# A graph-attention layer on one NeuronCore: the running sums move from a TensorE product and a ScalarE copy to two VectorE additions

## The chip, the core and the metric

The kernel runs on one core of one Trainium2 chip. The metric is the device time of one execution in microseconds (us). TensorE multiplies matrices, VectorE and ScalarE work on tiles in SBUF and PSUM, GpSimd issues the gathers, SyncE issues the other transfers. Each engine takes its instructions in order, and semaphores tie the engines together. In the profile they are called PE (PEld for its weight loads), DVE, ACT, POOL and SP (SPq for the queue that issues transfers).

## What is computed

A layer of 6250 nodes with 256 features (8 heads of 32) is the sum of a graph attention over 206250 edges sorted by destination, a linear-attention mixer, and after that eight experts. The stage that the change touches is the graph attention:

```
h_src, h_dst = h[src], h[dst]                      # h = layernorm(x) @ W.T, per edge
alpha = einsum(h_src, a_src) + einsum(h_dst, a_dst)
enc   = relu(edge_attr @ edge_W.T + edge_b)
alpha = leaky(alpha + sum(enc * h_dst))
ex    = exp(alpha - segment_max(alpha, dst)[dst])
out   = segment_sum(h_src * ex / segment_sum(ex, dst)[dst], dst)
```

## The kernel before

The program runs in stages: a start stage (`stage_start`), the mixer (`stage_kv`, `stage_mix`), the edge stage (`stage_edges`, 884 to 2835 us of the profile), `stage_combine` and `stage_experts`. The edge stage is unrolled by hand; nothing but the order of the code and the semaphores sets its order.

Edges are sorted by destination and cut into steps of 256 edges that touch 64 destination nodes. A **turn** is two steps (512 edges), there are 452 turns, and eight turns are a **window** (57 of them). At turn tau the front half of the work is done for tau, and the back half for d = tau - 12 (`LAG` is 11); the segment maximum and the exponentials of a finished window are worked out in its four following turns, one link of the chain in each (k = 0 to 3, k being the turn's place in the window).

In one turn the engines do this, in this order:

- TensorE: `spread_out` (L1666, L1670) spreads the destination rows over the edges with the one-hot tile `hot`; `encode` of the next turn (L1655) multiplies `w_rows` by `feat`, 30 rows (3 of ones for the bias, 27 of edge features in three bf16 parts); `aggregate(d)` (L1702, L1706) sums the weighted source rows `rows` per destination into `ps_a`; `reduce` (L1683) sums the products per head. In `aggregate`, step 0 of a turn goes on from what `sums` holds: the identity product L1702 first brings that tile (128x264, float32) into `ps_a`, except at k = 0.
- VectorE: `multiply` (L1851, two instructions), `spreader` (L1840, one-hot row tile `hot` of the next turn, 128x512 bf16), `weigh` (L1934), `add(d, 1)` (L1927, adds step 1 of `ps_a` to `sums`), and the links of the chain. `add(d, 0)` runs on VectorE for k = 0 alone, behind `rescale` (L1911, L1915).
- ScalarE: `rectify` (L1748), `put_back` (L1801, copies step 0 out of `ps_a` into `sums`, k > 0), `take_src` (L1759), `put_exps` (L1785), `one_hot` (L1793, L1795), and the exponentials of the chain.
- GpSimd: four gathers (L1643) for each turn whose rows were not gathered in earlier stages, 1312 in all; `released` holds each back until a turn has come. SyncE: `load_pair` (rows of `relb` and `feat` for two turns), two tiles of `table` a turn, and the loads of a window.

Which tile of `sums` a step adds to is a number read from `turns_w` into a register (`value_load`). `aggregate(d)` waits until both sums of d - 1 have been added (`added`), `reduce` waits for `multiply`, and `spread_out` stands behind `reduce` on TensorE.

## Time and profile before

| what | us |
|---|---|
| median of 3 runs (3996.34 to 3997.9) | 3997.06 |
| the profiled execution | 3997.66 |
| its span | 3995.8 |
| TensorE busy | 3671.8 (92%) |
| VectorE busy | 2677.7 (67%) |
| ScalarE busy | 2308.9 (58%) |
| GpSimd busy | 1792.8 (45%) |

The busy shares are means over stages with different limits. The profile also has the busy time by stretches of time, instructions in order of time, groups of instructions by line, and the clock that TensorE was granted, 1.00 being 2.4 GHz and 0.50 being 1.2 GHz.

### The profile page before, as it was taken

How to read it: one execution, taken by the hardware profiler on the slowest of the kernel's cores; microseconds unless marked ns; L12 is line 12 of the kernel's file. 1: busy time of each engine (PE TensorE's matmuls, PEld its weight loads, DVE VectorE, ACT ScalarE, POOL GpSimd, SP SyncE). 2: the span in 40 equal slices, each digit the busy share in tenths (PEclk: the TensorE clock that was granted, in tenths of full speed). 3: DMA queues.
4: the chain of work that ended last, by engine and by line, in shares of the span. 5: the costliest groups of instructions: out<-in, count | busy, mean ns of one | idle time of the engine just before them, and what ended most of it. 6: DMA issues, size and time to landing. Idle time of an engine off the chain costs nothing. (4 is left out here: it accounts for less than half of the span.)

```text
span 3995.8 us, 80425 instructions
## 1 busy us (share of the span) xinstructions
PE 3671.8 (92%) x22765; PEld 1800.7 (45%) x22765; DVE 2677.7 (67%) x5470; ACT 2308.9 (58%) x6074; POOL 1792.8 (45%) x1859
## 2 busy tenths in 40 slices
PE   5599989978999999999999999999699999999999
PEld 3344433323443344434444444443366666666666
DVE  8399933338898999989989898988533333332323
ACT  4466555545777777777777777777333333333332
POOL 4177766656666666666666666665000000000000
PEclk8799999987999999999999999999659999999999
DMA  7677767767777777777777777776220000000000
GB/s 217 168 216 217 217 217 229 231 196 222 214 228 217 222 221 223 224 220 218 227 221 223 219 229 218 224 222 196 66 74 1 10 10 0 9 9 0 9 9 9
DMA packets 378173, 629.74 MB, mean 158 GB/s; under 512 B 83912, under 2 KB 245063, under 8 KB 377536
## 3 DMA queue, kind: packets, MB, share of 16 engines
q1 hardware_dynamic: 277266, 356.80, 28.1%
q0 software_dynamic: 93408, 257.23, 24.3%
q10 hardware_dynamic: 7104, 11.01, 0.8%
q8 instruction: 179, 2.93, 0.3%
q14 instruction: 216, 1.77, 0.1%
HBM read 520.59 MB, written 104.12 MB: 156 GB/s over the span
## 5 line engine op out<-in xcount | busy, mean ns | idle before, releaser
L1643 POOL DMA_INDIRECT s_rows<-scratch_src_rows,s_idx_w x1312 | 1270.5, 968 | 656.5 <-issue 398.6
L1851 DVE SCALAR_TENSOR_TENSOR s_enc<-s_enc,s_a_dst,s_ps_d 128x512 f32<-128x512 f32 x904 | 633.2, 742 | 104.2 <-PE s_ps_d L1670 92.8
L2299 DVE SCALAR_TENSOR_TENSOR kx_y_all<-e_ps_o,kx_gate,kx_y_all 128x256 f32 (+1 forms) x392 | 173.6, 480 | 684.4 <-PE e_ps_o L2354 684.4
L1934 DVE TENSOR_TENSOR s_rows<-s_rows,s_ps_x 128x1024 f32<-128x1024 f32 x452 | 546.5, 1209 | 22.2 <-ACT s_a_w L1779 22.1
L1748 ACT ACTIVATE s_enc<-s_ps_f 128x1024 f32<-128x1024 f32 x452 | 460.2, 1018 | 160.2 <-PE s_ps_f L1655 152.4
L1706 PE MATMUL s_ps_a<-s_rows,s_hot_e 128*64 128x264 f32 x3616 | 536.6, 421 | 2.9 <-DVE s_rows L1934 2.9
L1793 ACT ACTIVATE s_hot_e<-k_iota_row,s_rel_w 128x64 f32<-128x64 f32 x1808 | 480.2, 338 | 0.0
L2313 ACT ACTIVATE ke_sums<-e_ps,kx_b,kx_g 128x448 f32<-128x448 f32 x224 | 162.1, 724 | 513.1 <-PE e_ps L2333 513.1
L1702 PE MATMUL s_ps_a<-ke_sums,k_ident 128*128 x790 | 292.4, 453 | 105.0 <-DVE ke_sums L1927 64.7
L2333 PE MATMUL e_ps<-kx_xT,ke_sums 128*128 (+1 forms) x896 | 348.1, 542 | 6.2 <-PEq L180 6.2
L2354 PE MATMUL e_ps_o<-ke_sums 128*128 128x256 f32 x1568 | 347.6, 379 | 0.0
L2343 PE MATMUL e_ps<-ke_sums 128*128 128x448 f32 x896 | 345.9, 539 | 0.0
L1706 PEld LDWEIGHTS s_ps_a<-s_rows,s_hot_e 128*64 128x64 f32 x3616 | 229.4, 142 | 251.3 <-issue 159.0
L2354 PEld LDWEIGHTS e_ps_o<-ke_sums 128*128 128x128 f32 x1568 | 297.8, 190 | 58.6 <-issue 20.9
L1683 PE MATMUL s_ps_s<-s_enc,s_head_sum 128*32 128x256 f32 x3616 | 304.7, 410 | 10.7 <-DVE s_enc L1851 4.0
L1801 ACT COPY ke_sums<-s_ps_a 128x264 f32 x395 | 148.0, 375 | 284.0 <-PE s_ps_a L1706 283.0
L1655 PE MATMUL s_ps_f<-s_feat,k_w_rows 30*128 30x512 bf16 x904 | 276.7, 386 | 19.7 <-DMA s_feat<-scratch_step_parts 19.2
L1195 POOL DMA_INDIRECT m_rows<-scratch_src_rows,m_idx x248 | 235.1, 948 | 117.9 <-issue 65.0
L1091 POOL DMA_INDIRECT n_rows<-scratch_src_rows,n_idx x248 | 235.4, 949 | 109.0 <-issue 71.9
L1670 PE MATMUL s_ps_d<-s_hot,s_table 128*128 128x256 bf16 x1808 | 283.6, 281 | 0.0
L1265 ACT ACTIVATE m_feats<-m_ps_s 124x896 f32<-124x896 f32 x224 | 193.3, 915 | 144.1 <-PE m_ps_s L1207 144.1
L2319 ACT ACTIVATE ke_sums<-e_ps,kx_b,kx_g 128x448 f32<-128x448 f32 x224 | 162.1, 724 | 174.6 <-PE e_ps L2343 174.6
(280 smaller groups left out, 5084.6 us busy)
## 6 DMA issues: line engine op xcount, KB each, us to landing
s_table<-scratch_dst_parts SPq DMA_DIRECT2D x904, 96.0 KB
s_rows<-scratch_pre_rows SPq DMA_DIRECT2D x124, 528.0 KB
s_relb<-scratch_rel_rows SPq DMA_DIRECT2D x226, 256.0 KB
scratch_pre_rows<-n_rows SPq DMA_DIRECT2D x62, 528.0 KB
scratch_pre_rows<-m_rows SPq DMA_DIRECT2D x62, 528.0 KB
s_rows<-scratch_src_rows,s_idx_w POOLq DMA_INDIRECT x1312
s_feat<-scratch_step_parts SPq DMA_DIRECT2D x226, 54.0 KB
s_pen_w<-scratch_pen_rows SPq DMA_DIRECT2D x228, 48.1 KB
```

What stands on the lines that cost most here:

```text
L1643: pool.indirect_dma_start(out=rows[:, d % R, m, :], out_offset=None, in_=scr["src_table"], in_offset=bass.IndirectOffsetOnAxis(ap=idx_w[:, ...
L1670: last = PE.matmul(ps_d[:, c, sub * GE:(sub + 1) * GE], table[:, u, sub, c * P:(c + 1) * P], hot[:, v, sub * GE:(sub + 1) * GE], start=Fal ...
L1683: last = PE.matmul(ps_s[32 * b:32 * (b + 1), :], head_sum[:, 28 - 4 * k:60 - 4 * k], enc[:, d % 2, c, sub * GE:(sub + 1) * GE], start=(k = ...
L1702: PE.matmul(ps_a[:, 0, 0:SRC_W], keep["ident"][:], sums[:, bass.ds(j, 1), :].rearrange("p o w -> p (o w)"), start=True, stop=False, skip_g ...
L1706: last = PE.matmul(ps_a[t * WN:(t + 1) * WN, sub, 0:SRC_W], hot_e[:, d % 3, 2 * sub + t, :], rows[:, d % R, 2 * sub + t, :], start=(sub == ...
L1748: A.activation(enc[:, d % 2], ps_f[:], ACT.Relu).then_inc(enc_made, 1)
L1793: A.activation(hot_e[:, d % 3, m, :], keep["iota_row"][:, 0:WN], ACT.Abs, bias=rel_w[:, w % 3, k * TD + m:k * TD + m + 1]).then_inc(dist_m ...
L1851: V.scalar_tensor_tensor(out=enc[:, d % 2, c, :], in0=enc[:, d % 2, c, :], scalar=a_dst[:, c:c + 1], in1=ps_d[:, c, :], op0=ALU.add, op1=A ...
L1934: V.tensor_tensor(v, v, by.unsqueeze(3).to_broadcast([P, TD, H, HD]), ALU.mult).then_inc(weighed, 1)
L2333: last = nc.tensor.matmul(ps[q][:, 0:W], w["W1"][:, e, c, m * P:(m + 1) * P], keep["xT"][:, c, bass.ds(i * 2 * W + hf * W, W)], start=(c = ...
L2343: last = nc.tensor.matmul(ps[q][:, 0:W], w["W2"][:, e, c, m * P:(m + 1) * P], h1[:, c, hf * W:(hf + 1) * W], start=(c == 0), stop=(c == 1))
L2354: last = nc.tensor.matmul(ps_o[q][:, r, :], h2[:, c, b * P:(b + 1) * P], w["Wo"][:, e, c, :], start=(c == 0), stop=(c == 1))
```

## The change

All of it is in the edge stage, but for the zeroed tiles.

- `aggregate` has no identity product any more; both steps of a turn come out of `ps_a` alone. `put_back` on ScalarE is gone, and `add(d, 0)` runs on VectorE in every turn, so that VectorE adds twice a turn and reads a register twice a turn.
- `spreader` works on pairs of turns: one 128x1024 instruction in every second turn, for a pair that is one to two turns ahead; `hot` has twice the size, and SyncE loads `relb` a pair ahead of `feat`.
- Steps of the chain leave VectorE: `starts` (the two small tiles `first`), `keep_run`, `fall` and `factors` (was L1911) run on ScalarE, and `both_ends` is one instruction and not two.
- `feat` and `w_rows` have 128 rows, of which 98 are zeros, so that `encode` contracts over 128 rows; `b_rows` and the tile of ones of the mixer's two bias products have 128 rows and not 3. The tiles are cleared once, in the start stage and at the head of the edge stage.

```diff
@@ aggregate (TensorE)
-                    if k > 0:
-                        j = pe.value_load(turns_w[0:1, w % 4, KS + 2 * k:KS + 2 * k + 1], min_val=0, max_val=NJ - 1)
...
-                    if k > 0:
-                        PE.matmul(ps_a[:, 0, 0:SRC_W], keep["ident"][:], sums[:, bass.ds(j, 1), :].rearrange("p o w -> p (o w)"),
-                                  start=True, stop=False, skip_group_check=True)
@@ ScalarE
+                def starts(w):
+                    act.wait_ge(hot_made, KW // 2 * w + 1)
+                    wait(act, fac_made, w - 2)
+                    h = hot[:, KW // 2 * w % 2, 0, 0:1]
+                    A.copy(first[:, w % 2, 0:1], h)
+                    A.activation(first[:, w % 2, 1:2], h, ACT.Identity, scale=-1.0, bias=one[:, 0:1]).then_inc(first_made, 1)
+                def keep_run(w):
...
+                def fall(w):
...
+                def factors(w):
+                    act.wait_ge(turned_, w + 1)
...
-                def put_back(d):
-                    w, k = win(d)
-                    j = act.value_load(turns_w[0:1, w % 4, KS + 2 * k:KS + 2 * k + 1], min_val=0, max_val=NJ - 1)
-                    act.wait_ge(summed[0], d + 1)
-                    A.copy(sums[:, bass.ds(j, 1), :].rearrange("p o w -> p (o w)"), ps_a[:, 0, 0:SRC_W]).then_inc(added, 1)
@@ VectorE
+                V.memset(feat[:], 0.0).then_inc(cleared, 1)
...
-                def spreader(d):
...
+                def spreader(g):
+                    dve.wait_ge(rel_in[g % RP], 16 * (g // RP + 1))
+                    wait(dve, spread[1], 2 * (g - 1))
+                    if g >= 2 and (g - 2) % (KW // 2) == 0:
+                        dve.wait_ge(first_made, (g - 2) // (KW // 2) + 1)
+                    V.tensor_scalar(hot[:, g % 2], relb[:, g % RP], p64[:, 0:1], None, ALU.is_equal).then_inc(hot_made, 1)
...
-                    if tau + 1 < D:
-                        spreader(tau + 1)
+                    if tau % 2 == 1 and tau + 3 < D:
+                        spreader((tau + 3) // 2)
...
-                    if tau >= LAG + 1 and win(tau - LAG - 1)[1] == 0:
+                    if tau >= LAG + 1:
                         add(tau - LAG - 1, 0)
```

TensorE, one plain turn (no link of the chain in it). Before:

```order
L1666 MATMUL s_ps_d<-s_hot,s_table 128x256 x4
L1670 MATMUL s_ps_d<-s_hot,s_table 128x256 x4
L1655 MATMUL s_ps_f<-s_feat,k_w_rows 128x512 x2
L1696 TENSOR_LOAD s_turns_w
L1696 ISA x2
L1702 ISA
L1702 MATMUL s_ps_a<-ke_sums,k_ident 128x264
L1706 MATMUL s_ps_a<-s_rows,s_hot_e 64x264 x4
L1683 MATMUL s_ps_s<-s_enc,s_head_sum 32x256 x4
```

The same turn after:

```order
L1674 MATMUL s_ps_d<-s_hot,s_table 128x256 x4
L1678 MATMUL s_ps_d<-s_hot,s_table 128x256 x4
L1663 MATMUL s_ps_f<-s_feat,k_w_rows 128x512 x2
L1709 MATMUL s_ps_a<-s_rows,s_hot_e 64x264 x4
L1691 MATMUL s_ps_s<-s_enc,s_head_sum 32x256 x4
```

The register read and the identity product are gone; nothing else moved.

VectorE, one plain turn. Before:

```order
L1851 SCALAR_TENSOR_TENSOR s_enc<-s_enc,s_a_dst,s_ps_d 128x512 x2
L1840 TENSOR_SCALAR s_hot<-s_relb,s_p 128x512
L1934 TENSOR_TENSOR s_rows<-s_rows,s_ps_x 128x32x32
L1920 TENSOR_LOAD s_turns_w
L1920 ISA x2
L1927 ISA
L1927 TENSOR_TENSOR ke_sums<-s_ps_a,ke_sums 128x264
```

An odd plain turn after (an even one has no L1868):

```order
L1874 SCALAR_TENSOR_TENSOR s_enc<-s_enc,s_a_dst,s_ps_d 128x512 x2
L1868 TENSOR_SCALAR s_hot<-s_relb,s_p 128x1024
L1937 TENSOR_LOAD s_turns_w
L1937 ISA x2
L1944 ISA
L1944 TENSOR_TENSOR ke_sums<-s_ps_a,ke_sums 128x264
L1951 TENSOR_TENSOR s_rows<-s_rows,s_ps_x 128x32x32
L1937 TENSOR_LOAD s_turns_w
L1937 ISA x2
L1944 ISA
L1944 TENSOR_TENSOR ke_sums<-s_ps_a,ke_sums 128x264
```

A second register read and a second addition now stand between the one-hot rows and L1951 (`weigh`).

## Rows read from the trace of the kernel before

**Rows 1.** The page: the span of the profiled execution.
```profile
span 3995.8 us, 80425 instructions
```

**Rows 2.** Busy time by stretch: a start of the stage, its middle, one clock dip.
```profile
core 0: us, PE busy (x) PEld busy (x) DVE busy (x) ACT busy (x) POOL busy (x), PEclk, DMA share, GB/s
...
904.00:925.30 21.30, 19.37 (x98) 5.72 (x97) 19.02 (x25) 5.96 (x11) 16.12 (x18) 0.50 0.80 235
...
1400.00:2600.00 1200.00, 1119.87 (x8434) 482.40 (x8432) 1088.67 (x2112) 927.00 (x2717) 803.31 (x832) 0.97 0.77 222
...
2044.87:2048.28 3.41, 3.41 (x21) 1.11 (x20) 1.94 (x6) 2.02 (x8) 2.80 (x3) 0.50 0.79 230
```

**Rows 3.** Timeline (start, length, work, idle before): TensorE in turns 15 and 451.
```profile
949.29 0.39 PE L1666 MATMUL s_ps_d<-s_hot,s_table 64*128 64x256 bf16 x4
...
2791.86 0.39 PE L1666 MATMUL s_ps_d<-s_hot,s_table 64*128 64x256 bf16 x4
```

**Rows 4.** Timeline: TensorE through one plain turn.
```profile
2033.74 0.39 PE L1666 MATMUL s_ps_d<-s_hot,s_table 64*128 64x256 bf16 x4
...
2035.13 0.71 PE L1702 MATMUL s_ps_a<-ke_sums,k_ident 128*128 x2
...
2035.78 1.11 PE L1706 MATMUL s_ps_a<-s_rows,s_hot_e 128*64 128x264 f32 x8
...
2036.82 0.64 PE L1683 MATMUL s_ps_s<-s_enc,s_head_sum 128*32 128x256 f32 x8
...
2037.39 0.39 PE L1666 MATMUL s_ps_d<-s_hot,s_table 64*128 64x256 bf16 x4
```

**Rows 5.** Timeline: VectorE through one plain turn, from the addition before it.
```profile
2027.16 0.43 DVE L1927 TENSOR_TENSOR ke_sums<-s_ps_a,ke_sums 128x264 f32 x1
2027.50 1.40 DVE L1851 SCALAR_TENSOR_TENSOR s_enc<-s_enc,s_a_dst,s_ps_d 128x512 f32<-128x512 f32 x2
...
2028.82 0.35 DVE L1840 TENSOR_SCALAR s_hot<-s_relb,s_p 128x512 bf16<-128x512 bf16 x1
2029.08 1.21 DVE L1934 TENSOR_TENSOR s_rows<-s_rows,s_ps_x 128x1024 f32<-128x1024 f32 x1
...
2030.21 0.43 DVE L1927 TENSOR_TENSOR ke_sums<-s_ps_a,ke_sums 128x264 f32 x1
...
2030.91 1.41 DVE L1851 SCALAR_TENSOR_TENSOR s_enc<-s_enc,s_a_dst,s_ps_d 128x512 f32<-128x512 f32 x2 [0.27 <-PE s_ps_d L1670]
```

**Rows 6.** Groups by line (busy us, mean ns, idle before): moved work, contraction rows, gathers.
```profile
L1643 POOL DMA_INDIRECT s_rows<-scratch_src_rows,s_idx_w x1312 | 1270.5, 968 | 656.5 <-issue 398.6 <-PE s_ps_a L1706 137.5 <-DVE s_hot L1840 55.5
...
L1655 PE MATMUL s_ps_f<-s_feat,k_w_rows 30*128 30x512 bf16 x904 | 276.7, 386 | 19.7 <-DMA s_feat<-scratch_step_parts 19.2
...
L906 PE MATMUL n_ps_qk<-kn_b_rows,kn_ones 3*128 3x512 bf16 x49 | 19.1, 389 | 0.3 <-DVE n_kp L1020 0.3
...
L1911 DVE TENSOR_SCALAR s_fac<-s_ps_x,s_first 128x8 f32<-128x8 f32 x56 | 15.6, 279 | 0.0
...
L1826 DVE MEMSET s_feat<- 3x2048 bf16 x1 | 1.8, 1765 | 5.6 <-PEq L180 5.6
```

**Rows 7.** Timeline: TensorE at half clock, in turn 6 and in the drain.
```profile
914.77 0.61 PE L1666 MATMUL s_ps_d<-s_hot,s_table 64*128 64x256 bf16 x4
...
918.72 0.61 PE L1666 MATMUL s_ps_d<-s_hot,s_table 64*128 64x256 bf16 x4
...
2804.38 1.24 PE L1702 MATMUL s_ps_a<-ke_sums,k_ident 128*128 x2 [0.84 <-DVE ke_sums L1927]
2805.55 2.03 PE L1706 MATMUL s_ps_a<-s_rows,s_hot_e 128*64 128x264 f32 x8
...
2808.41 1.24 PE L1702 MATMUL s_ps_a<-ke_sums,k_ident 128*128 x2 [0.84 <-DVE ke_sums L1927]
```

**Rows 8.** Timeline: one gather, and `encode` waiting for its load.
```profile
2002.70 0.95 POOL L1643 DMA_INDIRECT s_rows<-scratch_src_rows,s_idx_w  x1 [0.30 <-issue]
...
2043.09 0.60 PE L1655 MATMUL s_ps_f<-s_feat,k_w_rows 30*128 30x512 bf16 x2 [0.67 <-DMA s_feat<-scratch_step_parts]
```

More of the change, by code:

```diff
@@ L905, in project @@
                     wait(pe, q_made, i - 1)
-                    PE.matmul(ps_qk[u][:], keep["ones3"][:], keep["b_rows"][:, 0:2 * C], start=True, stop=False)
+                    PE.matmul(ps_qk[u][:], keep["ones_p"][:], keep["b_rows"][:, 0:2 * C], start=True, stop=False)
                     for c in range(2):
@@ L1227, in project @@
                     wait(pe, res_made, i)
[L1228 removed]
+                    PE.matmul(ps_o[:, 0:C], keep["ones_p"][:], keep["b_rows"][:, 2 * C:3 * C], start=True, stop=False)
                     for c in range(2):
@@ L1765, in leaked @@
                     A.activation(leak[:], ps_s[:], ACT.Copy, scale=SLOPE).then_inc(leak_made, 1)
+                def starts(w):
[5 more added lines that the diff above has]
+                def keep_run(w):
+                    u = w % 2
+                    act.wait_ge(chained, w + 1)
+                    A.copy(runs[:, 1 - u, 0:1], runs[:, u, KS:KS + 1]).then_inc(kept, 1)
+                def fall(w):
+                    act.wait_ge(carry_made, w + 1)
+                    wait(act, gain_made, w)
+                    A.activation(gap[:], carry[:, 0:1], ACT.Relu, scale=-1.0, bias=runs[:, w % 2, 2 * KS:2 * KS + 1]).then_inc(gap_made, 1)
+                def factors(w):
+                    act.wait_ge(turned_, w + 1)
+                    act.wait_ge(first_made, w + 1)
+                    wait(act, scaled, w - 1)
+                    A.activation(fac[:], ps_g, ACT.Identity, scale=first[:, w % 2, 0:1], bias=first[:, w % 2, 1:2]).then_inc(fac_made, 1)
                 def exponents(w):
                     act.wait_ge(gap_made, w + 1)
-                    A.activation(gain[:], gap[:], ACT.Exp).then_inc(gain_made, 1)
+                    A.activation(gain[:], gap[:], ACT.Exp, scale=-1.0).then_inc(gain_made, 1)
                     act.wait_ge(shifted, w + 1)
@@ L1807, in _ @@
                         leaked(w - 1)
+                    if k == 2 and 0 < w <= NW:
+                        keep_run(w - 1)
+                        fall(w - 1)
                     if k == 3 and 0 < w <= NW:
@@ L1817, in _ @@
                     if k == 3 and 0 < w <= NW:
+                        if w > 1:
+                            factors(w - 1)
                         by_edge(w - 1)
+                    if k == KW - 1 and tau + 1 < D:
+                        starts(w + 1)
                     if 0 <= tau - LAG < D:
@@ L1869, in both_ends @@
                     dve.wait_ge(seg_made, w + 1)
-                    for a, at in ((0, GE - 1), (1, 0)):
-                        last = V.tensor_scalar(ends[:, a, :], turn_of[:, a, :], seg[:, at:at + 1], None, ALU.mult)
-                    last.then_inc(ends_made, 1)
+                    v = seg[:]
+                    at = bass.AP(v.tensor, v.offset + GE - 1, [v.ap[0], [1 - GE, 2], [0, KS]])
+                    V.tensor_tensor(ends[:], turn_of[:], at, ALU.mult).then_inc(ends_made, 1)
                 def chain_runs(w):
@@ L1883, in carry_on @@
                     dve.wait_ge(chained, w + 1)
+                    wait(dve, gap_made, w)
                     V.tensor_tensor(carry[:], runs[:, u, 0:2 * KS], chain_w[:, u, 1, :], ALU.add).then_inc(carry_made, 1)
-                    V.tensor_copy(runs[:, 1 - u, 0:1], runs[:, u, KS:KS + 1]).then_inc(kept, 1)
-                def fall(w):
-                    dve.wait_ge(carry_made, w + 1)
-                    V.tensor_scalar(gap[:], carry[:, 0:1], runs[:, w % 2, 2 * KS:2 * KS + 1], 0.0, ALU.subtract, ALU.min).then_inc(gap_made, 1)
                 def pick(w):
@@ L1909, in rescale @@
                 def rescale(w, j):
-                    dve.wait_ge(a_made, w + 1)
-                    V.tensor_scalar(fac[:], ps_g, first[:, w % 2, 0:1], first[:, w % 2, 1:2], ALU.mult, ALU.add).then_inc(fac_made, 1)
                     dve.wait_ge(fac_made, w)
@@ L1966, in _ @@
                         back(w - 1)
-                    elif chain == 1:
-                        fall(w - 1)
                     elif chain == 2:
```

57 lines of the change are left out of this document (27 added, 30 removed).

## The prediction

> **What bounds the kernel now.** I read the busy time by stretch first, then the order in time of single turns, then the groups by line. The span is 3995.8 us [rows 1]; the profiled execution took 3997.66, so 1.9 us lie around the span, and the median of the runs is 0.6 below it. Nearly half of the span is the edge stage. In its middle TensorE is busy for 1119.87 of 1200 us (93%) and VectorE for 1088.67 (91%) [rows 2]: both are close to the bound, and the question is which one waits. From the start of turn 15 (949.29) to that of turn 451 (2791.86) are 1842.6 us [rows 3], 4.23 us a turn, and with eight turns to a window 33.8 us a window, 54.5 of them.
>
> A plain turn on TensorE takes 37.39 - 33.74 = 3.65 us without a gap: spreading and encoding 1.39, identity product 0.65, aggregate 1.04, reduce 0.57 [rows 4]. A plain turn on VectorE is 1.32 for the two multiplications, 0.26 for the one-hot rows, 1.13 for the weighing and 0.34 for one addition, together 3.05, and then it waits for the spread product of the next turn [rows 5]. So TensorE sets plain turns. In the turns that hold links of the chain VectorE is the later one, and TensorE waits for it. One place more: in some windows TensorE is granted 0.50 for one short stretch, and all of that stretch (the last row) is matmuls at half speed [rows 2], right after it had waited for a load and for the chain [rows 8].
>
> **The change, part by part.**
>
> Identity product: 0.65 us less in seven of eight turns on TensorE, so a plain turn needs 3.00. Nothing else there gets longer: contraction over 3, 30 and 128 rows costs by row alone what the columns cost, 389 ns for 3 rows and 386 for 30 at 512 columns [rows 6]. I take 0 for the padding.
>
> Second addition: VectorE gets 7 more of 0.34 a window, +2.4 us. ScalarE loses as many copies, which lie beside other work and give nothing, since it is busy for 927.00 of 1200 us [rows 2]. The register read in front of each addition lies under the multiplications or the weighing, except at k = 3, where two additions stand side by side; there I put 0.3.
>
> One-hot rows of two turns: four instructions of 1024 columns a window for eight of 512. An instruction step is 0.26 at 512 [rows 5]. The one at 1024 lies between 0.26 (all fixed cost) and 0.52 (none); no row excludes either end. I take the middle, 0.39, so 2.1 becomes 1.6: -0.5 a window, with bounds -1.0 and 0. The Trainium skill (VectorE: DVE Perf Modes, What auto-detection actually checks) says that a one-source bf16 operation between SBUF tiles moves four elements a cycle; estimated from that page's 0.96 GHz, 512 more columns would add 0.13 and give the same 0.39.
>
> Links moved to ScalarE: six instruction groups, of which the largest is the 279 ns of L1911 [rows 6], leave VectorE or (both ends of a window) become one instruction. Between 0.06 and 0.39 us of VectorE's time each; together I take -1.1 a window, with bounds -0.6 (only half of what they cost was on the path) and -1.4. On ScalarE they wait for events that are over by their place in the order. `factors` is an exception: it stands in front of the copy that the weighing at k = 3 waits for, and delays it by about its own 0.28 at most. VectorE comes there later by one addition and its register read (0.34 + 0.3), so this is hidden; without that cover it would be 0.28 a window, 15 us in all.
>
> The new sum for a window: VectorE is busy for 0.907 of 33.8 = 30.7 us now [rows 2, 3]. 30.7 + 2.4 - 0.5 - 1.1 = 31.5. TensorE needs 33.8 x 0.93 = 31.5 - 7 x 0.65 = 26.9, so **VectorE becomes the bound in every turn**: plain turns alternate between 3.13 and 3.52, for TensorE's 3.00. I give VectorE 0.3 of waits (the register read at k = 3) and take **31.8 us a window**. The loop that could bind closes in time: reduce, spreading and encoding end 0.57 + 1.39 after the multiplications, before the turn's last addition; aggregate then takes 1.04 while the multiplications (1.32) of the next turn run, so its first sum is there when the added `add(d, 0)` comes.
>
> 54.5 x (33.8 - 31.8) = **-109**.
>
> Drain, the 12 turns after the last front half: 4.03 us a turn at half clock, because both sums, the identity product (1.17) and aggregate (2.03) follow one another [rows 7]. After: aggregate's first half about 1.3, add 0.34, weigh 1.13, add 0.43, that is 3.2. Ten such turns give **-8**; bounds 0 and -10.
>
> Start, the first 15 turns, with no aggregate: 3.95 us a turn at 0.50 [rows 7]. No identity product is in them, so TensorE's work does not change; bounds 0 and -6 (if the clock rises earlier), I take **-2**. Cleared tiles: a second clearing of 2048 columns at the head of the stage, 1.77 [rows 6], and half as many columns again in the start stage, **+3**; bounds +1 and +3.
>
> Sum: 3997.7 - 109 - 8 - 2 + 3 = 3881.7 for the profiled execution, so **3881** for the median.
>
> **The rivals.**
>
> A. *Feeding becomes the bound.* Loads keep their length while turns get shorter. For it: `encode` already waits 0.67 us for its load at k = 1 [rows 8], behind the loads of a window on SyncE, and GpSimd issues 1312 gathers at 0.95 + 0.30 = 1.25 [rows 6, 8], 23.2 of them or 29.0 us a window, which leaves 2.8 of 31.8. Against it: that wait stands where TensorE then waits for the chain anyway, and GpSimd's pauses now add up to 656.5 us [rows 6]. If both cost together 1.2 us a window: 33.0, -44 - 7 = 3946. The Trainium skill (SBUF — State Buffer, Who interferes with whom) says that VectorE in its two-port modes shuts GpSimd out for a whole instruction, and the one-hot rows can be in such a mode; rows 6 show 55.5 us in which a gather waited for L1840, though that is also the wait written in `released`. Four blocks of about 0.4 a window would bring GpSimd to 30.6, still inside 31.8.
>
> B. *Slower: TensorE falls to half clock.* TensorE will be busy for 26.9 of 31.8 us (85%) where it was for 93%. At 0.50 the work of a turn is 3.95 less a wait of 0.4, and 2.0 for aggregate, 5.5 us [rows 7], against 3.97 for the mean VectorE-bound turn. It decides from (4.23 - 3.97)/(5.5 - 3.97) = 17% of the turns at half clock. With half of them: 4.74 a turn, 37.9 a window, +223 - 7, so 4213. Against it: the matmuls that stay fill the array as before, and the padded encode fills more of it. A stretch at 0.50 is on record with TensorE busy for 91% of it (19.37 of 21.30 us), in turns of spreading, encoding and small reduces alone, and the clock stays up as soon as aggregate, which stays, is in the turns [rows 2]. The Trainium skill (TensorE: Matmul & The Clock Gate, Part 1) ties the clock to how busy the engine was lately; by that the fall from 93% to 85% would be the risk, and this row shows that the busy share alone does not tell. The dips that remain should cost less than now, since TensorE has 0.3 us and more to spare in each turn.
>
> C. *No difference*: some order of waits that I overlook takes back what the identity product gives. A window would have to get 2 us of new waits: 3990 to 4005.
>
> D. *More*: additions and one-hot rows at their lower bounds, 31.1 a window: -147, 3843.
>
> **How the numbers follow.** Forecast (3850 to 3915) 0.62; A (3915 to 3960) 0.17; something between A and no difference, still faster, 0.06; D (under 3850) 0.04; C 0.03; B and other losses 0.08. The range that leaves out B, C, the smaller part of A and of D runs from 3846 to 3946. A measurement of this kernel can tell about 0.2%, or 8 us, from no change: faster 0.89, same 0.03, slower 0.08.
>
> **What the profile after would show.** VectorE busy for 97% or more of the stage's middle, and TensorE for about 85% with the clock at 0.97 to 1.00; a window of 31.8 us between starts of the spread product eight turns apart; plain turns that alternate between about 3.5 (with one-hot rows) and 3.1 to 3.2; VectorE's rows in plain turns without an idle time for TensorE; a one-hot step of 0.39. Wrong would be the forecast if VectorE's idle time before L1874 named the spread product or a load (A), if the clock in the middle were under 0.9 (B), or if the addition's step were well over 0.34 because the register read shows through.

## The result, and the profile after

The changed kernel takes **3900.5 us** (median of 4 runs, 3887.3 to 3902.3) against 3997.0 for the kernel before on the same chip: a ratio of 0.9751, 95% interval 0.973 to 0.9773. The forecast was 3881 (3846 to 3946). Its profiled execution took 3902.3, so 95.3 us less than the profiled one of before; 4.3 of them went ahead of the edge stage, 97.2 inside it, and 6.2 came back behind it, in the combine stage (117.4 us before, 123.5 now), whose code is the same. From the end of the edge stage to the start of the experts the granted clock is 0.61 before and 0.56 now; among the kernels below nopad has 115.3 at 0.59 there, and both traces of the changed kernel have the longer time. What decides it is not shown.

The 4.3 us ahead of the edge stage go with another part of the change, the 128 rows of the mixer's bias product: `stage_mix` took 360.8 us and takes 356.3. Of the kernels below and these two, on chips of this speed, the six whose bias product has 128 rows take 355.9 to 358.4 there, and the four where it has 3 rows 360.8 to 364.8. From the product ahead of a bias product to the one behind its group (bias and projection) are 1.62 us before and 1.55 now, medians of 49.

The page, its span and the slices of VectorE and of the granted clock (answers to [rows 1]):

```profile
span 3900.5 us, 77375 instructions
...
DVE  8399923338999999999999999998633333333333
...
PEclk8799989997999999999999999998579999999999
```

Busy time by stretch, the same middle of the stage as in [rows 2], and one clock dip:

```profile
core 0: us, PE busy (x) PEld busy (x) DVE busy (x) ACT busy (x) POOL busy (x), PEclk, DMA share, GB/s
1400.00:2600.00 1200.00, 1007.73 (x8282) 456.75 (x8281) 1146.32 (x2094) 898.79 (x2767) 835.04 (x868) 0.97 0.81 232
1536.66:1540.08 3.42, 3.42 (x22) 1.08 (x18) 2.60 (x5) 2.24 (x10) 2.81 (x3) 0.50 0.77 218
```

TensorE fell from 93% to 84%, VectorE rose from 91% to 95.5%. The roles are as forecast, but not the 97% that the prediction asked for: VectorE still stands still for 4.5% of the stretch.

Timeline, TensorE, the spread product that opens turn 15 and the one that opens turn 451 (counted from 0):

```profile
950.44 0.39 PE L1674 MATMUL s_ps_d<-s_hot,s_table 64*128 64x256 bf16 x4
...
2697.00 0.39 PE L1674 MATMUL s_ps_d<-s_hot,s_table 64*128 64x256 bf16 x4
```

That is 1746.6 us, or **32.05 a window**. Here a slip of the prediction shows: the row at 949.29 of [rows 3] is turn 13, and turn 15 of before starts at 956.59 (timeline, kernel before):

```profile
956.59 0.39 PE L1666 MATMUL s_ps_d<-s_hot,s_table 64*128 64x256 bf16 x4
```

Before's windows took 1835.3 / 54.5 = 33.67, not 33.8, so the stretch in question got 88.7 us shorter, where the forecast of 109 held some 7 us of miscount.

A window's length now has two kinds. Taken at every eighth start of the spread product, 54 windows, beside the recorded stretches at 0.50: 30 windows without one take 31.03 on average (the shortest 30.7), and 24 windows with one take 33.4. Before, 27 without took 32.74 and 27 with took 34.6.

Timeline, TensorE, then VectorE, through two plain turns of the kernel after (columns: start, length, work, idle before; answers to [rows 4] and [rows 5]):

```profile
1554.33 0.39 PE L1674 MATMUL s_ps_d<-s_hot,s_table 64*128 64x256 bf16 x4
...
1555.10 0.59 PE L1663 MATMUL s_ps_f<-s_feat,k_w_rows 128*128 128x512 bf16 x2
1555.97 1.11 PE L1709 MATMUL s_ps_a<-s_rows,s_hot_e 128*64 128x264 f32 x8 [0.27 <-DVE ke_sums L1944]
1557.28 0.64 PE L1691 MATMUL s_ps_s<-s_enc,s_head_sum 128*32 128x256 f32 x8 [0.20 <-DVE s_enc L1874]
1557.85 0.39 PE L1674 MATMUL s_ps_d<-s_hot,s_table 64*128 64x256 bf16 x4
...
1560.98 0.39 PE L1674 MATMUL s_ps_d<-s_hot,s_table 64*128 64x256 bf16 x4
```

```profile
1558.52 0.42 DVE L1944 TENSOR_TENSOR ke_sums<-s_ps_a,ke_sums 128x264 f32 x1
1558.87 1.40 DVE L1874 SCALAR_TENSOR_TENSOR s_enc<-s_enc,s_a_dst,s_ps_d 128x512 f32<-128x512 f32 x2
1560.18 0.48 DVE L1868 TENSOR_SCALAR s_hot<-s_relb,s_p 128x1024 bf16<-128x1024 bf16 x1
1560.57 0.43 DVE L1944 TENSOR_TENSOR ke_sums<-s_ps_a,ke_sums 128x264 f32 x1
1560.91 1.21 DVE L1951 TENSOR_TENSOR s_rows<-s_rows,s_ps_x 128x1024 f32<-128x1024 f32 x1
```

The two turns take 3.52 and 3.13, the alternation that the forecast wrote down; VectorE has no idle time in them, and TensorE waits for it. The one-hot step is 1560.57 - 1560.18 = 0.39 and the addition 0.34. Now the groups by line, with idle time and what ended it:

```profile
L1651 POOL DMA_INDIRECT s_rows<-scratch_src_rows,s_idx_w x1312 | 1265.6, 965 | 570.2 <-issue 384.9 <-PE s_ps_a L1709 132.4 <-DMA s_idx_w<-scratch_edge_idx 21.8
L1874 DVE SCALAR_TENSOR_TENSOR s_enc<-s_enc,s_a_dst,s_ps_d 128x512 f32<-128x512 f32 x904 | 630.7, 738 | 20.2 <-PE s_ps_d L1678 20.2
...
L1663 PE MATMUL s_ps_f<-s_feat,k_w_rows 128*128 128x512 bf16 x904 | 281.1, 394 | 132.4 <-DMA s_feat<-scratch_step_parts 130.7 <-ACT s_hot_e L1821 1.5
```

`encode` waited 19.2 us for its feature rows in the whole stage before [rows 6]; it waits **130.7** now. Of the 2.0 us of it in a window, 1.68 fall in the turn k = 1. And in this kernel such a wait is what stands ahead of a clock dip. Timeline, TensorE, around the dip at 1536.66:

```profile
1532.37 0.61 PE L1678 MATMUL s_ps_d<-s_hot,s_table 128*128 128x256 bf16 x4
1535.23 0.61 PE L1663 MATMUL s_ps_f<-s_feat,k_w_rows 128*128 128x512 bf16 x2 [2.25 <-DMA s_feat<-scratch_step_parts]
...
1537.20 1.08 PE L1691 MATMUL s_ps_s<-s_enc,s_head_sum 128*32 128x256 f32 x8
1538.21 0.61 PE L1674 MATMUL s_ps_d<-s_hot,s_table 64*128 64x256 bf16 x4
```

After 2.25 us of standing still come products at the 1.2 GHz level (0.61 for the four that take 0.39 at 2.4 GHz). In the 5 us ahead of the 22 dips that begin between 1020 and 2640 TensorE stands idle for 2.41 us on average, 2.14 of them in waits for feature rows, and each of the 22 has such a wait; any 5 us of that stretch hold 0.76 and 0.32. In the kernel before, 27 dips of the same stretch follow 1.1 us of idle time, with only 0.10 of it for feature rows; 22 of them, too, begin in the turn k = 1.

### The profile page after: what moved, and what is told of

Same layout as the page of the kernel before. It is cut to its first block and busy times, and to the rows that moved or that the text cites. A ratio compares the mean times of both kernels' runs of the same rounds, so it can differ in the third digit from the quotient of the medians.

```text
span 3900.5 us, 77375 instructions
## 1 busy us (share of the span) xinstructions
PE 3398.0 (87%) x21975; PEld 1729.4 (44%) x21975; DVE 2692.1 (69%) x5301; ACT 2204.8 (57%) x5963; POOL 1789.8 (46%) x1859
## 5 line engine op out<-in xcount | busy, mean ns | idle before, releaser
L1874 DVE SCALAR_TENSOR_TENSOR s_enc<-s_enc,s_a_dst,s_ps_d 128x512 f32<-128x512 f32 x904 | 630.7, 738 | 20.2 <-PE s_ps_d L1678 20.2
L1709 PE MATMUL s_ps_a<-s_rows,s_hot_e 128*64 128x264 f32 x3616 | 527.6, 413 | 90.2 <-DVE ke_sums L1944 59.5
L1951 DVE TENSOR_TENSOR s_rows<-s_rows,s_ps_x 128x1024 f32<-128x1024 f32 x452 | 545.1, 1206 | 7.9 <-ACT s_a_w L1805 6.2
L1944 DVE TENSOR_TENSOR ke_sums<-s_ps_a,ke_sums 128x264 f32 x904 | 381.2, 422 | 57.1 <-PE s_ps_a L1709 39.0
L1663 PE MATMUL s_ps_f<-s_feat,k_w_rows 128*128 128x512 bf16 x904 | 281.1, 394 | 132.4 <-DMA s_feat<-scratch_step_parts 130.7
L1709 PEld LDWEIGHTS s_ps_a<-s_rows,s_hot_e 128*64 128x64 f32 x3616 | 243.8, 140 | 319.9 <-DVE s_rows L1951 185.3
L1691 PE MATMUL s_ps_s<-s_enc,s_head_sum 128*32 128x256 f32 x3616 | 299.9, 402 | 80.2 <-DVE s_enc L1874 46.5
L2359 PEld LDWEIGHTS e_ps<-ke_sums 128*128 128x128 f32 x896 | 170.2, 190 | 166.5 <-issue 166.5
```

The source lines that it names most:

```text
L1691: last = PE.matmul(ps_s[32 * b:32 * (b + 1), :], head_sum[:, 28 - 4 * k:60 - 4 * k], enc[:, d % 2, c, sub * GE:(sub + 1) * GE], start=(k = ...
L1709: last = PE.matmul(ps_a[t * WN:(t + 1) * WN, sub, 0:SRC_W], hot_e[:, d % 3, 2 * sub + t, :], rows[:, d % R, 2 * sub + t, :], start=True, s ...
L1874: V.scalar_tensor_tensor(out=enc[:, d % 2, c, :], in0=enc[:, d % 2, c, :], scalar=a_dst[:, c:c + 1], in1=ps_d[:, c, :], op0=ALU.add, op1=A ...
L1944: V.tensor_tensor(y, ps_a[:, sub, 0:SRC_W], y, ALU.add).then_inc(added, 1)
L1951: V.tensor_tensor(v, v, by.unsqueeze(3).to_broadcast([P, TD, H, HD]), ALU.mult).then_inc(weighed, 1)
L2359: last = nc.tensor.matmul(ps[q][:, 0:W], w["W2"][:, e, c, m * P:(m + 1) * P], h1[:, c, hf * W:(hf + 1) * W], start=(c == 0), stop=(c == 1))
```

## The experiments

Three theories compete for the 20 us between forecast and measurement, and for the 89 us that the windows did give. *Sum*: VectorE's work sets the window, as the prediction adds it up. *Feeding*: the windows wait for loads. *Clock*: the array's work, product and zero rows, decides how often TensorE falls to 0.50. The kernels ran on three chips. On two of them the kernel before takes 4000.7 and 3997.9 us (ratios are always to that kernel on the same chip); on the third it takes 4828.8, and what ran there stands at the end of this section. In the table ctl_after, win_late, nopad and before_noident ran on the first, the other four on the second. "Windows", "with dip" and "half" are worked out from the trace of each kernel as above: mean window length, how many of 54 have a stretch at 0.50, and how much of it per window. They come from one execution each, whose time differs from the median by 4.5 to 11.7 us in four kernels (4028.2 for before_noident, 3997.1 for before_noident_pad2, 3910.2 for ident_back2, 3893.7 for ctl_after), so steps between windows are good to some 0.2 us.

| kernel | median us | ratio, 95% interval | window | with dip | half, us |
|---|---|---|---|---|---|
| before | 4000.7 / 3997.9 | 1 | 33.68 | 27 | 1.96 |
| before_noident | 4016.5 | 1.0036 [1.0024, 1.0049] | 34.16 | 54 | 5.88 |
| before_pad2 | 3953.3 | 0.9893 [0.9871, 0.9916] | 32.85 | 22 | 1.39 |
| before_noident_pad2 | 3991.2 | 0.9987 [0.997, 1.0005] | 33.68 | 24 | 1.52 |
| ident_back2 | 3917.6 | 0.9807 [0.9776, 0.9838] | 32.29 | 13 | 0.95 |
| nopad | 3911.0 | 0.9775 [0.9758, 0.9791] | 32.22 | 35 | 3.73 |
| ctl_after (the change) | 3889.3 | 0.9709 [0.9689, 0.973] | 31.92 | 21 | 1.52 |
| win_late_nopad | 3865.3 | 0.9668 [0.9648, 0.9687] | 31.48 | 14 | 1.01 |
| win_late | 3848.7 | 0.962 [0.9603, 0.9636] | 31.28 | 4 | 0.25 |

### The change again, as the control

> The changed kernel once more, beside the others on the same chip. Both theories expect 0.975 of the kernel before (3887 to 3902 us), with windows of 30.7 us where encode finds its load in place and none of the window at half clock, and 32.0 us as the mean.

The changed kernel, unaltered, so that its neighbours on that chip have their own measure: 3889.3 us, ratio 0.9709. That is 0.4% better than in the first comparison, with 21 instead of 24 dips; the change's effect is -2.5 to -2.9%.

### Feeding: the window's loads issued later

SyncE issues, in the turn k = 0, first the feature rows of the current pair, then the tables, then six loads of a window (one of `rel_w`, four of `pen_w`, one of `chain_w`; the expectations count seven), and behind them, with the tables between, the next feature rows. Here the six are issued at k = 5:

```diff
-                    if k == 0:
+                    if k == 5 or d == D - 1:
                         load_window(w)
```

(At the last turn, D - 1, the short window at the end gets its loads.) A third buffer for feature rows, which might take the wait itself away, wasn't tried.

> The changed kernel, with the seven loads of a window (one rel_w, four pen_w, one chain_w) issued by SyncE at k = 5 of their window and not at k = 0; nothing else. Their data are needed eight turns later, the feature rows of the turns k = 2 and 3 in three turns. Theory F (late feature rows are the cause of both the waits and most half-clock stretches): encode's wait for its load falls from 131 us in all to under 20, the half-clock stretches in the steady part go from 24 windows to under 8, the mean window from 32.05 to about 30.9, so 54.5 x 1.15 = 63 us less than the changed kernel, about 3835. Theory G (the transfers themselves are slow, since DMA queues are fuller at 232 GB/s): the wait stays at more than half, and the time within 20 us of 3900. Theory H (the clock falls by itself because TensorE has less work): the load wait goes, but the half-clock stretches stay at about 24 windows and take about 0.46 of their length, so 3870 or so.

Measured: **3848.7 us, ratio 0.962**, 41 us under the control and the best of all kernels. Busy time by stretch and the encode's group, kernel win_late:

```profile
1400.00:2600.00 1200.00, 1006.01 (x8357) 463.42 (x8507) 1174.49 (x2149) 926.09 (x2840) 862.67 (x891) 1.00 0.82 238
```

```profile
L1663 PE MATMUL s_ps_f<-s_feat,k_w_rows 128*128 128x512 bf16 x680 | 224.6, 385 | 98.9 <-DMA s_feat<-scratch_step_parts 85.7 <-issue 0.7
```

VectorE is busy for 98% and the clock is 1.00. The wait for feature rows sank from 126.4 us in the control to 85.7 and was split among k = 1, 5 and 7 (0.33, 0.58 and 0.28 us a window, where k = 1 alone had 1.67), and the windows with a dip went from 21 to 4. That is theory F for the dips and theory G for the wait, of which more than half stayed, and the time lies between F and H: later loads split the waits more than they removed them. The wait also grows as the turns get shorter, from 19.2 us before to 46.5 in before_pad2 and 79.0 in ident_back2. So feeding costs the changed kernel at least 0.64 us a window (31.92 - 31.28), the dips that it brings included; this is rival A of the prediction, in part.

### Clock: the zero rows taken back

```diff
-                        last = PE.matmul(ps_f[:, c, :], w_rows[:, c * P:(c + 1) * P], feat[:, d // 2 % RP, d % 2, :], start=True, stop=True)
+                        last = PE.matmul(ps_f[:, c, :], w_rows[0:FR, c * P:(c + 1) * P], feat[0:FR, d // 2 % RP, d % 2, :], start=True, stop=True)
```

> The changed kernel, but encode contracts over the 30 rows that hold data and not over 128; the tiles are still cleared. If the zero rows help the clock, it is granted less here: more windows with a stretch at 0.50 than the 24 of the changed kernel, up to all, and 1 to 2 us a window more, 3930 to 4000. If they do nothing, 3900 within 10 us and as many stretches.

3911.0 us against 3889.3 for the control, 0.56% slower, with 35 windows that dip instead of 21. That is less than the 30 us or more that the expectation asked for, and clear of the runs' spread: the mean granted clock is 0.928 to 0.936 in the four runs and 0.946 to 0.953 in the control's. Busy time by stretch, kernel nopad:

```profile
1400.00:2600.00 1200.00, 1052.12 (x8302) 446.29 (x8301) 1148.81 (x2092) 901.22 (x2768) 842.45 (x868) 0.95 0.79 232
```

The windows without a dip are no longer than in the control (30.85 against 31.0); the loss goes with the clock, 0.95 for 0.98. The zero rows are worth some 20 us here, where the prediction took 0.

The same edit on top of win_late tells whether a dip needs the wait, the small product, or both:

> The changed kernel with the window loads issued at the window's sixth turn, as in win_late, and with the encode product over the 30 real rows alone, as in nopad. Theory (a half-clock stretch needs both a wait and the small product; with shorter waits at the encode the rows matter less): 5 to 15 of 54 windows dip, a window of 31.4 to 31.8 us, 3855 to 3880 us, ratio 0.964 to 0.970. Rival (the zero rows act by themselves, as 35 against 21 windows in nopad and its control): 20 or more windows dip, 31.9 us or more a window, 3880 to 3895 us, ratio 0.970 to 0.974. Third: no dips to speak of, 3849 us as win_late, ratio 0.962.

Measured 3865.3, ratio 0.9668, 14 windows with a dip, 31.48 a window: the first theory in all its numbers. Late loads and zero rows each lower the count (35 with neither, 21 with the rows, 14 with the late loads, 4 with both). Each lowers it with or without the other.

### The product alone

Only the identity product and ScalarE's copy leave the kernel before; VectorE adds both steps' sums:

```diff
-                    if k > 0:
-                        PE.matmul(ps_a[:, 0, 0:SRC_W], keep["ident"][:], sums[:, bass.ds(j, 1), :].rearrange("p o w -> p (o w)"),
-                                  start=True, stop=False, skip_group_check=True)
...
-                                             start=(sub == 1 or k == 0), stop=True, skip_group_check=True)
+                                             start=True, stop=True, skip_group_check=True)
...
-                    if tau >= LAG + 1 and win(tau - LAG - 1)[1] == 0:
+                    if tau >= LAG + 1:
```

> The kernel before with only the identity product and the ScalarE copy taken out and both steps added on VectorE; one-hot rows, chain links and the 30 rows as before. VectorE then carries 2.4 us a window more than before, and 1.6 more than in the changed kernel: windows of 32.3 at best, against 32.7 before. By the forecast's sums the identity product alone is worth little, 3970 to 3990, and the gain of the change needs the relief of VectorE. If TensorE's 0.65 a turn were the whole story it would be at 3900 or below. If half clock spreads (less matmul work, no zero rows), 4000 or more.

**Slower, by 0.36%**: 4016.5 us, and every one of the 54 windows dips. Busy time by stretch, then the timeline of TensorE in one dip, kernel before_noident:

```profile
1400.00:2600.00 1200.00, 1029.03 (x7815) 437.82 (x7812) 1131.69 (x2320) 819.40 (x2427) 779.19 (x816) 0.91 0.76 219
```

```profile
1453.35 1.03 PE L1655 MATMUL s_ps_f<-s_feat,k_w_rows 30*128 30x512 bf16 x2
...
1454.58 2.03 PE L1701 MATMUL s_ps_a<-s_rows,s_hot_e 128*64 128x264 f32 x8
```

This is rival B's mechanism (aggregate takes 2.03 in a dip for 1.11), once the prediction's main step is taken alone; it is not the whole of the loss, as the next kernel shows. The clock fell to 0.91 while TensorE was busy for 86% of the stretch (1029 of 1200). Then with the zero rows added to it:

> The kernel before, with the identity product and ScalarE's copy taken out (VectorE adds both steps' sums) and with the encode product's zero rows added; the same kernel as before_noident_pad, whose run fell on a chip where the kernel before itself took 4829 us. Theory (zero rows keep the clock up that the missing product let fall): the half-clock stretches, 5.9 us a window in before_noident, shrink to under 3 us, a window takes 33.0 to 33.8 us, the time is 3950 to 3995 us, ratio 0.988 to 0.999. Rival (the clock hangs on the waits alone, zero rows do nothing): all 54 windows still dip, about 5.9 us of each, window 34.1 us, ratio 1.002 to 1.006.

3991.2 us, ratio 0.9987, 1.52 us of half clock a window, window 33.68: all four inside the theory's numbers. 24 windows dip instead of 54, and the mean granted clock of the ten runs is 0.949 to 0.955 instead of 0.915 to 0.926. Busy time by stretch, kernel before_noident_pad2:

```profile
1400.00:2600.00 1200.00, 953.99 (x7758) 448.60 (x7898) 1148.55 (x2354) 825.73 (x2453) 792.70 (x828) 0.98 0.77 221
```

TensorE's modelled busy share is *lower*, 79%, and its granted clock higher, 0.98. The Trainium skill (TensorE: Matmul & The Clock Gate, Part 1) ties the clock to how busy the engine was lately. By the busy rows alone the trace disagrees: 86% gave 0.91 and 79% gave 0.98. The edit between the two is the zero rows alone. They fill more of the array, and they also take away gaps between products that count as busy here (next kernel); no run tells which of the two the clock answers to.

And yet 3991 is no gain to speak of, and 38 us more than the same kernel with its identity product (3953.3, next). VectorE is at 95.7% there: the window is its work, 0.957 x 33.68 = 32.2.

### The zero rows alone

```diff
-        feat = s.sb("feat", [FR, RP, 2, ED], BF16)
+        feat = s.sb("feat", [P, RP, 2, ED], BF16)
...
+                V.memset(feat[:], 0.0).then_inc(cleared, 1)
...
+                V.memset(keep["w_rows"][:], 0.0)
```

> The kernel before with nothing but the encode product's zero rows added; the same kernel as before_pad. Theory (the half-clock stretches of the kernel before, in 27 of its 54 windows at 34.6 against 32.7 us, are the part that the zero rows act on): at most 10 windows with such a stretch, a window of 32.8 to 33.2 us, 3950 to 3970 us, ratio 0.988 to 0.994. Rival (zero rows change nothing where the identity product is kept): 3990 to 4000 us, ratio 0.998 to 1.001, and about 27 windows with a stretch.

**3953.3 us, -1.07%**, with a part of the change that the prediction put at 0. The time is where the theory had it, but its reason is at most half right: 22 windows still dip, not 10 or fewer, and the windows *without* a dip got shorter too, from 32.74 to 32.23. The timelines show why. TensorE's weight loads (PEld) in a plain turn, kernel before, of which [rows 4] show the products in another such turn:

```profile
1593.25 0.33 PEld L1670 LDWEIGHTS s_ps_d<-s_hot,s_table 128*128 128x128 bf16 x4 [0.21 <-issue]
1593.79 0.11 PEld L1655 LDWEIGHTS s_ps_f<-s_feat,k_w_rows 30*128 30x128 bf16 x2 [0.21 <-issue]
1594.32 0.30 PEld L1702 LDWEIGHTS s_ps_a<-ke_sums,k_ident 128*128 128x128 f32 x2 [0.42 <-issue]
```

Weight loads, then products, in a plain turn of kernel before_pad2 (in the row at 1577.10 one of the two products has no record; its weight load is at 1576.78):

```profile
1576.43 0.33 PEld L1671 LDWEIGHTS s_ps_d<-s_hot,s_table 128*128 128x128 bf16 x4 [0.21 <-issue]
1576.78 0.21 PEld L1656 LDWEIGHTS s_ps_f<-s_feat,k_w_rows 128*128 128x128 bf16 x2
1577.10 0.41 PEld L1703 LDWEIGHTS s_ps_a<-ke_sums,k_ident 128*128 128x128 f32 x2
1577.85 0.64 PEld L1707 LDWEIGHTS s_ps_a<-s_rows,s_hot_e 128*64 128x64 f32 x8 [0.34 <-issue]
```

```profile
1576.12 0.39 PE L1667 MATMUL s_ps_d<-s_hot,s_table 64*128 64x256 bf16 x4
1576.44 0.61 PE L1671 MATMUL s_ps_d<-s_hot,s_table 128*128 128x256 bf16 x4
1577.10 0.38 PE L1656 MATMUL s_ps_f<-s_feat,k_w_rows 128*128 128x512 bf16 x1
1577.32 0.61 PE L1703 MATMUL s_ps_a<-ke_sums,k_ident 128*128 x2
1577.86 1.11 PE L1707 MATMUL s_ps_a<-s_rows,s_hot_e 128*64 128x264 f32 x8
...
1579.47 0.39 PE L1667 MATMUL s_ps_d<-s_hot,s_table 64*128 64x256 bf16 x4
```

In the plain turn of before, no weights are loaded while a product of another number of rows runs: the load for the 30-row product starts at 1593.79 with its product, 0.54 after the 128-row products began, and the one for the identity product at 1594.32, again with its product. With 128 rows in all three, the encode's load starts 0.35 after the first of the 128-row spread products' loads (1576.78 - 1576.43), and the loads go without a gap from one product into the next ("0.21 <-issue" and "0.42 <-issue" are gone). The identity product starts 1.20 after the turn's first spread product instead of 1.40 (1577.32 - 1576.12; 1.39 in [rows 4]), aggregate 0.54 behind it instead of 0.65 [rows 4], and the plain turn takes **3.35 instead of 3.65**. Every "busy" row of the prediction held all the same (379 to 394 ns on average for one product of 512 columns, with 30 rows before and with 128 in before_pad2 and after); what the rows cost lies between the products. Equal rows alone are not enough: aggregate's load, 128 rows but 64 columns, still starts only with its own product (1577.85, 0.34 of idle time ahead of it). The Trainium skill (TensorEngine Tiling (Array Packing), Key Properties) says that a change of tiling mode drains the engine. If a product of 30 rows beside products of 128 is such a change, this trace agrees: the padding saves some 0.20 us at two changes, and 0.10 more inside the identity product, whose first weights came late.

### The product put back into the changed kernel

Everything of the change except the product's removal: zero rows, one-hot rows of two turns, links on ScalarE. The edit is the three pieces of before_noident with + and - exchanged.

> The changed kernel with the identity product and ScalarE's copy put back (VectorE adds the second step's sums alone), the zero rows, the two-turn hot rows and the links on ScalarE kept; the same kernel as ident_back. Theory (in the changed kernel VectorE's second add, 0.34 us in 7 of 8 turns or 2.4 us a window, is mostly hidden under the waits for feature rows, and the product's 0.4 us a turn on TensorE costs about as much): a window of 31.5 to 32.3 us, within 0.5% of the changed kernel, 3880 to 3920 us, ratio 0.970 to 0.980. Rival (as in the sum of the prediction, VectorE sets the window and the second add costs all of its 2.4 us): windows near 29.8 us, 3770 to 3800 us, ratio 0.943 to 0.951.

3917.6 us, ratio 0.9807; the window of 32.29 is at the theory's edge, the ratio just above it, and the rival's 3770 to 3800 is out. Timeline, TensorE, one plain turn of ident_back2, from one spread product to the next reduce (the turn ends at 1559.98):

```profile
1556.63 0.39 PE L1674 MATMUL s_ps_d<-s_hot,s_table 64*128 64x256 bf16 x4
...
1557.83 0.61 PE L1710 MATMUL s_ps_a<-ke_sums,k_ident 128*128 x2
1558.37 1.11 PE L1714 MATMUL s_ps_a<-s_rows,s_hot_e 128*64 128x264 f32 x8
1559.41 0.64 PE L1691 MATMUL s_ps_s<-s_enc,s_head_sum 128*32 128x256 f32 x8
```

A plain turn takes 3.35 with the product, and (3.52 + 3.13) / 2 = 3.33 without it. **In plain turns the product's removal gives nothing once the encode has its zero rows.** What it gives, 0.3 of a window (32.29 to about 32.0) and 5 us in the drain (53.5 to 48.5), lies elsewhere. By the medians, with 0.9807 against 0.9709 and 0.9751 for the changed kernel, it is 22 to 39 us in all, so 0.3 to 0.6 of a window.

Only two of a window's eight turns, k = 6 and 7, are such plain turns. Mean length of each turn in the windows without a dip, from start to start of the spread product:

| kernel | k = 0 | 1 | 2 | 3 | 4 | 5 | 6 | 7 | sum |
|---|---|---|---|---|---|---|---|---|---|
| before | 4.10 | 4.98 | 3.80 | 4.61 | 3.19 | 4.75 | 3.65 | 3.65 | 32.74 |
| before_noident_pad2 | 4.79 | 4.94 | 3.85 | 4.84 | 3.87 | 4.33 | 3.39 | 3.39 | 33.39 |
| before_pad2 | 3.80 | 5.48 | 3.88 | 4.35 | 3.23 | 4.77 | 3.35 | 3.35 | 32.23 |
| ident_back2 | 3.82 | 5.32 | 3.88 | 4.47 | 3.47 | 4.06 | 3.35 | 3.35 | 31.73 |
| after | 3.79 | 4.76 | 3.73 | 4.71 | 3.76 | 3.60 | 3.53 | 3.13 | 31.03 |

More than half of the change's 1.7 us in these windows lies in k = 5, where aggregate stands behind VectorE's sums. Timeline, TensorE at k = 5, kernel before (the identity product, with 0.64 of the array's time between sums and aggregate), then after:

```profile
1657.84 0.71 PE L1702 MATMUL s_ps_a<-ke_sums,k_ident 128*128 x2 [1.04 <-DVE ke_sums L1927]
```

```profile
1583.91 1.11 PE L1709 MATMUL s_ps_a<-s_rows,s_hot_e 128*64 128x264 f32 x8 [0.34 <-DVE ke_sums L1944]
```

The removal takes 0.56 off k = 1 and 0.46 off k = 5 and puts 0.24 and 0.29 on k = 3 and 4: 0.7 in windows without a dip. More windows dip without the product (24 and 21 for 13), and that takes back some 0.4.

Read along one path, the windows say what each step is worth: 33.68, with zero rows 32.85 (-0.83), with one-hot pairs and links 32.29 (-0.56), without the product 32.0 (-0.3; -0.3 to -0.6 by the medians). Read along the other: 33.68, without the product 34.16 (+0.48; the traced run is a long one, the median says about +0.4), with zero rows 33.68 (-0.48), with one-hot pairs and links 32.0 (-1.7). With the zero rows in place the removal costs 0.8 where VectorE still has its old work (32.85 to 33.68), and pays 0.3 to 0.6 where it hasn't. One-hot pairs and links were moved together in every kernel; what each gives is open.

### Four kernels on a slower chip

These ran on a chip where the kernel before took 4828.8 us (4815 to 4848). The experts stage took its 1015 us there too, but windows took 44 to 45.5 us in the four kernels traced; groups by line, GpSimd's gathers, kernel before_pad:

```profile
L1644 POOL DMA_INDIRECT s_rows<-scratch_src_rows,s_idx_w x1312 | 1269.1, 967 | 1264.8 <-PE s_ps_a L1707 538.7 <-issue 476.9 <-remote 185.3
```

Idle time of 1264.8 us ahead of the gathers instead of 656.5 [rows 6], part of it "remote", and 167 GB/s in the stage's middle where the same kernel (before_pad2) moves 227: transfers are slow there, all windows but two at most dip in every kernel, and the four ratios lie within 1% of one another, each with an interval 0.65 to 0.85% wide. A window there waits for other things than on the other chips, so these runs decide nothing about the theories, and the same kernels as before_pad, before_noident_pad and ident_back stand above, on another chip, as before_pad2, before_noident_pad2 and ident_back2.

> The kernel before with encode's zero rows alone (128 rows contracted, tiles cleared). In the kernel before 27 of 54 windows have a half-clock stretch and are 34.6 us long against 32.7. If zero rows keep the clock up, most of these go: up to 1.0 us a window, 55 us, 3945 to 3965. If the clock answers to waits alone, nothing changes: within 8 us of before.

Measured: 4771.2 us, ratio 0.9873 [0.983, 0.9915].

> The kernel before without the identity product, both steps added on VectorE, and with encode's zero rows; one-hot rows and chain links as before. Without the zero rows every window had 5.9 us at half clock and took 34.2. If the zero rows hold the clock, the windows become VectorE-bound at about 32.3 and the time 3910 to 3940; the rest to the changed kernel (31.9) is then what the relief of VectorE gives. If they don't, 34 a window and about 4010.

4789.0, ratio 0.991 [0.9877, 0.9944].

> The changed kernel with the identity product and the ScalarE copy put back (one-hot rows of two turns, moved chain links and zero rows stay). TensorE's plain turns are 3.65 again. Bound by TensorE with the clock up: windows of 32.5, about 3945. It shows what the relief of VectorE and the zero rows give without the trade: if near 3900, the identity product was not needed to go.

4755.5, ratio 0.9849 [0.9807, 0.989].

The fourth is the changed kernel with a window's six loads spread, two at k = 2 and one at each of k = 3 to 6 (the edit in `load_window` itself, which splits it by `part`, isn't shown):

```diff
-                    if k == 0:
-                        load_window(w)
+                    if k == 2:
+                        load_window(w, 0)
+                    if 3 <= k <= 6 and KW * w + 6 < D:
+                        load_window(w, k - 2)
```

> The changed kernel with the loads of a window spread by SyncE: rel_w and chain_w at k = 2, one pen_w at each of k = 3 to 6. With all seven at k = 5 the windows took 31.28 us, 4 of 54 had a half-clock stretch, and encode still waited 1.4 us a window, now at k = 5 and 7. If lateness of loads behind a block of seven is the rest, the waits go and windows take 30.5 to 30.8: 3810 to 3825. If transfers are late by themselves, 3840 to 3850 as with the block.

4745.4, ratio 0.9817 [0.9784, 0.9849]. Whether spreading the loads beats win_late on a chip with the usual transfers stays open.

## Why the prediction was nearly right

The time was 19.5 us above the forecast and inside the range; the sign was right. By its steps:

- **VectorE becomes the bound.** Right in kind, but for the waits: no idle time on VectorE in plain turns, its wait for the spread product down to 20.2 us in all, and the alternation of 3.52 and 3.13 as written down. Its *work* was over-estimated: 0.955 x 32.05 = 30.6 a window against 31.5. The base was 0.907 x 33.67 = 30.5 instead of 30.7 (the miscounted turn). The second additions cost 32.2 - 30.3 = 1.95 (before_noident_pad2 against before_pad2) or 30.6 - 29.0 = 1.6 (ctl_after against ident_back2), not 2.4. A likely reason, argued and not shown: seven times 0.34 assumes that each is added whole, while before a part of an instruction's end (0.43 long for a step of 0.34) lay in idle time and counted as busy. One-hot pairs and links together gave 32.2 - 30.6 = 1.6, as forecast (0.5 + 1.1); their split was not tried apart, only the one-hot step itself is seen at 0.39.
- **0.3 us of waits a window** was the term that failed. Between starts it is 32.05 - 30.6 = 1.4: some 0.4 in windows without a dip (31.03), and 1.0 more through dips. Too much work (0.9) and too few waits (1.1) nearly cancelled, so 31.8 came close to 32.05 by the meeting of two errors.
- **Rival A, feeding.** It was drawn up with the right place (k = 1, behind a window's loads on SyncE) and set aside because "that wait stands where TensorE then waits for the chain anyway". It was hidden before, and is not hidden now: 19.2 us became 130.7. It cost at least the 0.64 a window that win_late gave back, of the 1.2 that A put on it, while the windows without it were shorter than the forecast's.
- **Padding 0.** The step that failed outright: a term put at nothing. The argument was from the length of a product with 3, 30 and 128 rows, which is right, and says nothing of the gap at a change of rows. Alone the zero rows of `encode` give 44 us. In the changed kernel the gap no longer counts, and they give 22 us (3911.0 to 3889.3), with the clock. Those of the mixer's bias product go with 4 us more, ahead of the edge stage.
- **Identity product 0.65 a turn.** Its length was right, and it did leave TensorE; but that it carries the gain was wrong. In the two plain turns it was TensorE's bound of 3.65 that had to go, 0.30 of it went by the zero rows, and VectorE, at 3.33, stood right below the 3.35 that were left. At k = 5 it counted in another way, which the sum did not have: it stood between VectorE's sums and aggregate.
- **Rival B, half clock.** Its mechanism exists (before_noident), and the argument against it held by an edit that the text only touched: "the padded encode fills more of it". Without the zero rows the part meant as the gain loses 16 us against the kernel before; with them, and VectorE's work unrelieved, it loses 38 against before_pad2, by VectorE and not by the clock (33.4 for 32.2 in windows without a dip). Even in the changed kernel 21 to 24 windows dip where 13 do with the product.
- **Drain and start.** Predicted -8 and -2; measured 55.1 to 48.5, so -6.6, and turn 0 to turn 15 69.8 to 66.1, so -3.7. Timeline, TensorE, in the drain (answer to [rows 7]):

```profile
2703.03 1.11 PE L1709 MATMUL s_ps_a<-s_rows,s_hot_e 128*64 128x264 f32 x8 [1.39 <-DVE s_rows L1951]
2705.85 1.11 PE L1709 MATMUL s_ps_a<-s_rows,s_hot_e 128*64 128x264 f32 x8 [1.71 <-DVE ke_sums L1944]
2708.76 2.03 PE L1709 MATMUL s_ps_a<-s_rows,s_hot_e 128*64 128x264 f32 x8 [1.80 <-ACT s_rows L1811]
```

  Aggregate is at half clock (2.02 or 2.03) in nine of its ten rows from there on, and the turns of 2.8 to 2.9 between these rows are shorter than the 3.2 of the forecast where the clock is still up. Clearing: the stage's first spread product comes 10.8 after its start for 8.9, +1.9 for the +3.
- **GpSimd.** The Trainium skill (SBUF — State Buffer, Who interferes with whom) was weighed against the pairs of one-hot rows. The gathers' row shows no idle time ended by L1868 among its largest, where L1840 had 55.5 us, and a gather's mean length is 965 ns for 968, so here the longer one-hot instruction did no harm that these rows show.

## What to carry to other kernels

A product's row tells what it costs, and not what the change to it costs: read the starts of the weight loads beside the products, and where a load begins only with its own product, ask whether both neighbours can have the same number of rows (equal columns weren't tried). When work is taken from one of two engines that are both over 90% busy, cost the next bound first; here, in plain turns, the other engine stood 0.3 us below, and a cheaper edit reached the same place. A short wait for a load that is "hidden anyway" should be costed again as if its cover were gone, with the clock dip that follows it.

## What the runs showed of the hardware

- Products with 30 rows between products with 128 (before against before_pad2): 0.20 us lost over two changes, and 0.10 in the next product (plain turn 3.65 against 3.35), with no difference in the length of the 512-column products.
- Thirty rows filled up with zeros to 128 raised the granted clock: 0.91 to 0.98 without the product, 0.95 to 0.98 in the changed kernel, with the modelled busy share lower (86% to 79%, 88% to 83%).
- TensorE stood idle for 2.41 us, on average, in the 5 us ahead of a stretch at 1.2 GHz in the changed kernel, and for 1.1 in the kernel before, there for other things than loads. Such a stretch has no fixed price: a linear fit of window length to its length gives 0.48 us per us before, 0.55 and 0.60 in the two traces of the changed kernel, 0.33 in nopad and 0.19 in before_noident_pad2.
- One of three chips moved 167 GB/s in the edge stage of the kernel with zero rows alone, where another moved 227, and took 21% longer for the kernel before.
